# Long runs per partition: stacked operands of the causal attention, and spill and read-back of the relative heads

## The reference, cut to what matters

```
AC = einsum("bhld,bhmd->bhlm", q + u_bias, k)
BD = einsum("bhld,hrd->bhlr", q + v_bias, r)      # r: 2L-1 relative positions
attn = softmax((AC + rel_shift(BD)) / sqrt(8))
```

## Time and profile before

| what | value |
|---|---|
| runs of the kernel, not profiled | 1694.71, 1694.87, 1704.96 us; median 1694.87 us |
| profiled execution | 1699.04 us, of which the span from the first to the last instruction is 1697.2 us |
| PE, DVE, ACT, POOL busy | 87%, 73%, 66%, 26% of the span |
| mean granted TensorE clock | 0.948 of full speed |
| DMA moved | 272.97 MB in 154904 packets |
| causal attention | about 45 to 645 us of the span |
| windowed layers | about 645 to 1150 us |
| relative heads and last feed-forward | about 1150 to 1697 us |

### The profile page before, as it was taken

How to read it: one execution, slowest core, us unless ns; L and a number is a source line. 1 busy time by engine, 2 the same in 40 slices (tenths; PEclk the granted TensorE clock), 3 DMA queues, 4 the chain that set the end, 5 groups by cost and what they waited for, 6 DMA issues and landing times. The chain is left out here.

```text
span 1697.2 us, 36694 instructions
## 1 busy us (share of the span) xinstructions
PE 1473.9 (87%) x12580; PEld 938.1 (55%) x12580; DVE 1234.0 (73%) x3703; ACT 1119.9 (66%) x2657; POOL 440.1 (26%) x442
## 2 busy tenths in 40 slices
PE   4688998989989885588888888769999999999996
PEld 2255555556555553366666666646555555555564
DVE  4367777777777765688888788663877878878755
ACT  1267676776767761567777677627888787887742
POOL 0333333333333313454544444330000000000001
PEclk9599999999999997899999999877999999999998
DMA  1677777788777745111001110007999999999920
GB/s 41 163 185 194 188 186 197 185 194 190 186 186 189 194 108 187 22 30 31 19 20 31 25 27 19 12 13 219 324 315 315 309 314 300 313 314 302 292 73 25
DMA packets 154904, 272.97 MB, mean 161 GB/s; under 512 B 27920, under 2 KB 31200, under 8 KB 154592
## 3 DMA queue, kind: packets, MB, share of 16 engines
q1 hardware_dynamic: 154720, 270.63, 56.3%
HBM read 148.03 MB, written 112.98 MB: 154 GB/s over the span
## 5 line engine op out<-in xcount | busy, mean ns | idle before, releaser
L519 ACT ACTIVATE a_Pm<-a_Pm,a_nm 128x272 f32<-128x272 f32 (+3 forms) x512 | 266.7, 570 | 167.3 <-DVE a_nm L441 166.7
L441 DVE CUSTOM_DVE_ANT_0 a_Pm<-ps,a_mask 128x272 f32<-128x272 f32 (+3 forms) x512 | 237.7, 503 | 92.3 <-PE ps L358 90.8
L1768 ACT COPY r_BD<-ps 128x320 f32<-128x320 f32 x512 | 200.4, 428 | 92.1 <-PE ps L1621 46.7
L1895 DVE CUSTOM_DVE_ANT_0 r_Sx<-ps,r_Sx 128x512 f32<-128x512 f32 x256 | 176.8, 691 | 108.8 <-PE ps L1634 107.2
L1621 PE MATMUL ps<-r_R,r_qv 32*128 32x320 f32 x1024 | 234.2, 498 | 3.2 <-ACT r_BD L1768 2.3
L358 PE MATMUL ps<-a_Kst,a_Qst 128*128 128x272 f32 (+4 forms) x640 | 200.6, 409 | 15.4 <-DMA a_Kst<-bounce 15.1
L1634 PE MATMUL ps<-r_K,r_qu 32*128 32x256 f32 x1024 | 199.7, 436 | 3.4 <-DVE r_nb L1895 3.4
L358 PEld LDWEIGHTS ps<-a_Kst,a_Qst 128*128 128x128 f32 x640 | 113.4, 193 | 146.3 <-issue 62.6
L1775 ACT ACTIVATE r_Sx<-r_Sx,r_nb 128x512 f32<-128x512 f32 x256 | 187.6, 733 | 7.9 <-DVE r_nb L1895 7.9
L1904 DVE COPY r_PT<-ps 128x512 f32<-128x512 f32 x256 | 175.9, 687 | 4.6 <-PE ps L1644 4.0
L373 PE MATMUL ps<-m_ident,a_Pm 128*128 128x128 f32 x1280 | 170.5, 278 | 1.6 <-ACT a_Pm L519 0.7
(11 more groups left out here) (204 smaller groups left out, 2745.9 us busy)
## 6 DMA issues: line engine op xcount, KB each, us to landing
spill<-r_BD SPq DMA_DIRECT2D x256, 288.0 KB, 5.0
r_Sx<-spill SPq DMA_DIRECT2D x128, 512.0 KB, 5.7
a_Kst<-bounce SPq DMA_DIRECT2D x128, 264.0 KB, 4.9
a_Qst<-bounce SPq DMA_DIRECT2D x128, 256.0 KB, 4.6
bounce<-a_kh SPq DMA_DIRECT2D x32, 264.0 KB, 3.5
bounce<-a_kl SPq DMA_DIRECT2D x32, 264.0 KB, 4.1
bounce<-a_qh SPq DMA_DIRECT2D x32, 256.0 KB, 5.7
bounce<-a_ql SPq DMA_DIRECT2D x32, 256.0 KB, 6.0
```

The costliest lines, as they stand in the source:

```text
L441: nc.vector.tensor_tensor_reduce(out=Pm[:, u % 2, qt, 0:w], in0=S[:, S_of[qt]:S_of[qt] + w], in1=mask[:, N + AV - w:N + AV], scale=-SCALE, ...
L519: nc.scalar.activation(row, row, ACT.Exp, scale=-1.0, bias=nm[:, u % 2, qt:qt + 1]).then_inc(exp_done, 1)
L1768: nc.scalar.copy(BD[:, m % BUFS, j, HW * half:HW * half + HW], ps[:, BDB[k % 3], 0:HW]).then_inc(bd_ev, 1)
L1895: nc.vector.tensor_tensor_reduce(out=row, in0=ps[:, AC + n % 2, :], in1=row, scale=-SCALE, scalar=-BIG, op0=ALU.add, op1=ALU.min, accum_ou ...
```

## The change

Both DRAM buffers get a layout in which what one partition reads or writes lies together.

- Stacks: the DRAM buffer is now (2, 32 features, 4 heads, N) and no longer (2, 128, 528). The stacked tiles Qst and Kst have the sequence outside the head. A write goes through a view "c h n -> h c n" of the buffer: its outermost dimension has 4 entries, the next 32. Each of the four reads now has one run of 8192 or 8448 bytes per partition.
- Spill: one DMA writes all 2 x 640 columns of the 128 partitions (5120 bytes each), and the read takes one run of 640 + 512 elements (4608 bytes) per partition. wr rises by 16 instead of 32 per pair. Sx grows to 1152 elements per slot; to make room, yb and the output tile of the norm are laid over the last quarter of xT.
- First keys: first_transposes goes to bank TB + 1 and waits for VectorE's evd instead of ScalarE's eva; the wait for p0_ev moves from the transposes of bank TB (last of a unit) to those of bank TB + 1 (first of a unit).

```diff
-    Qst = [s.sb(f"Qst{i}", [P, GH, NB, N], F32R) for i in range(2)]
-    Kst = [s.sb(f"Kst{i}", [P, GH, NB, KN], F32R) for i in range(2)]
+    Qst = [s.sb(f"Qst{i}", [P, NB, GH, N], F32R) for i in range(2)]
+    Kst = [s.sb(f"Kst{i}", [P, NB, GH, KN], F32R) for i in range(2)]
...
-    bounce = [[nc.dram_tensor(f"bounce{k}{m}", (2, P, KN), F32, kind="Internal").ap() for m in range(4)] for k in range(2)]
+    bounce = [[nc.dram_tensor(f"bounce{k}{m}", (2, AD, GH, (N, KN)[m % 2]), F32, kind="Internal").ap() for m in range(4)] for k in range(2)]
...
-                width_ = (N, KN)[m % 2]
-                    sp.dma_start(bounce[st % 2][m][j, :, 0:width_], src[:, i].bitcast(F32)).then_inc(bounced, 16)
+                    sp.dma_start(bounce[st % 2][m][j].rearrange("c h n -> h c n"), src[:, i].bitcast(F32)).then_inc(bounced, 16)
-                    sp.dma_start(dst[st % 2][32 * block:32 * block + 32, :, i].bitcast(F32),
-                                 bounce[st % 2][m][j, :, 0:width_].rearrange("(h c) n -> c h n", h=GH)).then_inc(stk[st % 2][i], 16)
+                    sp.dma_start(dst[st % 2][32 * block:32 * block + 32, i].rearrange("c h n -> c (h n)").bitcast(F32),
+                                 bounce[st % 2][m][j].rearrange("c h n -> c (h n)")).then_inc(stk[st % 2][i], 16)
...
-                        ins = nc.tensor.matmul(S[:, lo:lo + w], q[:, h, i, P * qt:P * qt + P], k[:, h, i, at:at + w],
+                        ins = nc.tensor.matmul(S[:, lo:lo + w], q[:, i, h, P * qt:P * qt + P], k[:, i, h, at:at + w],
...
+                    if u >= GH and u % GH == 1:
+                        pe.wait_ge(p0_ev, u // GH)
-                if k == 0 and u >= GH and u % GH == 1:
-                    pe.wait_ge(p0_ev, u // GH)
...
-                pe.wait_ge(eva, 2 * min(GH * (bb + 1) + 1, UNITS))
+                pe.wait_ge(evd, min(GH * (bb + 1) + 1, UNITS))
-                    ins = nc.tensor.transpose(ps[:, TB, P * qt:P * qt + P], P0[:, bb % 2, qt, :], c["ident"][:])
+                    ins = nc.tensor.transpose(ps[:, TB + 1, P * qt:P * qt + P], P0[:, bb % 2, qt, :], c["ident"][:])
...
-                nc.vector.tensor_copy(P0T[:], ps[:, TB, :]).then_inc(p0_ev, 1)
+                nc.vector.tensor_copy(P0T[:], ps[:, TB + 1, :]).then_inc(p0_ev, 1)
...
-    def __init__(self, s, name):
+    def __init__(self, s, name, out=None):
-        self.out = s.sb(name + "_out", [P, NT, D])
+        self.out = s.sb(name + "_out", [P, NT, D]) if out is None else out
...
-    spill = [nc.dram_tensor(f"spill{k}", (2, P, BW), F32, kind="Internal").ap() for k in range(SCRATCH)]
+    spill = [nc.dram_tensor(f"spill{k}", (P, 2 * BW), F32, kind="Internal").ap() for k in range(SCRATCH)]
...
-    Sx = s.sb("Sx", [P, SCRATCH, 2, N])
+    Sx = s.sb("Sx", [P, SCRATCH, BW + N])
...
-    yb = s.sb("yb", [P, NT, D])
-    nrm = Norm(s, "n")
+    yb = xT[:, B - 1].rearrange("p (t n) -> p t n", t=NT)
+    nrm = Norm(s, "n", out=yb)
...
-    HW, HP2 = BW // 2, P // 2
+    HW = BW // 2
...
-                    rows_of = spill[k % SCRATCH].rearrange("t p n -> p t n")
-                    sp.dma_start(rows_of[0:HP2, :, HP2:BW], BD[0:HP2, k % BUFS, :, HP2:BW]).then_inc(wr[k % BUFS], 16)
-                    sp.dma_start(rows_of[HP2:P, :, 0:BW - HP2], BD[HP2:P, k % BUFS, :, 0:BW - HP2]).then_inc(wr[k % BUFS], 16)
+                    sp.dma_start(spill[k % SCRATCH], BD[:, k % BUFS].rearrange("p t n -> p (t n)")).then_inc(wr[k % BUFS], 16)
-                    sp.wait_ge(wr[m % BUFS], 32 * (m // BUFS + 1))
+                    sp.wait_ge(wr[m % BUFS], 16 * (m // BUFS + 1))
-                    skew = bass.AP(tensor=a.tensor, offset=P - 1, ap=[[BW - 1, P], [P * BW, 2], [1, N]])
+                    skew = bass.AP(tensor=a.tensor, offset=P - 1, ap=[[2 * BW - 1, P], [1, BW + N]])
...
-                    ins = nc.tensor.transpose(ps[:, TB + n % 2, P * j:P * j + P], Sx[:, n // 2 % SCRATCH, n % 2, P * j:P * j + P],
+                    ins = nc.tensor.transpose(ps[:, TB + n % 2, P * j:P * j + P], Sx[:, n // 2 % SCRATCH, BW * (n % 2) + P * j:BW * (n % 2) + P * j + P],
...
-                    act.wait_ge(wr[m % BUFS], 32 * (m // BUFS))
+                    act.wait_ge(wr[m % BUFS], 16 * (m // BUFS))
-                row = Sx[:, n // 2 % SCRATCH, n % 2, :]
+                row = Sx[:, n // 2 % SCRATCH, BW * (n % 2):BW * (n % 2) + N]
...
-                        act.wait_ge(wr[k], 32 * len(range(k, PAIRS, BUFS)))
+                        act.wait_ge(wr[k], 16 * len(range(k, PAIRS, BUFS)))
...
-                row = Sx[:, m % SCRATCH, n % 2, :]
+                row = Sx[:, m % SCRATCH, BW * (n % 2):BW * (n % 2) + N]
...
-                    nrm.apply(nc, link, nrm.out, yb)
+                    nrm.apply(nc, link, yb, yb)
-                    nc.vector.tensor_tensor(xs, xs, nrm.out[:], ALU.add).then_inc(x_done, 1)
+                    nc.vector.tensor_tensor(xs, xs, yb, ALU.add).then_inc(x_done, 1)
```

## The result

The changed kernel takes 1972.94 us (median of 4 runs, 1968.76 to 1984.96) beside 1698.08 us for the kernel before on the same chip: a ratio of 1.1624, 95% interval 1.1555 to 1.1694. The forecast was 1953 us, slower. In the profiled executions the span goes from 1697.2 to 1967.0 us, +269.8; the forecast had +258.

What follows compares the result with a forecast made beforehand. SP's loop of stack writes, landing and reads was taken to bound the causal attention, TensorE the relative heads. Stack writes +266 us and spill -8 us made +258 on 1694.87, so 1953 us; range 1810 to 2025.

Steps and rivals of the forecast that it cites:

- SP's loop paces the attention, not TensorE: Causal attention: SP's loop of writes, landing and reads sets the stage, 8.98 us a stack; TensorE nearly keeps pace.
- 15.2 us of TensorE's four units: Causal attention: TensorE's time for four units without its stalls, from 17.97 - 1.3 - 1.5.
- The rival at 1600 us: Stacks: writes over 16 engines, reads at 378 GB/s, TensorE then binds: -87 us; chance 0.07.
- Part one: First transposes: the 44 us stall for ScalarE goes but turns into waiting for data; worth 0.
- Part two: Stack reads: runs of 8 KB still fill 32 partitions, so 4.9 us a stack stays; at most 12 us gained.
- the rival of fast reads (1843 us): Stacks: four engines write, but long runs lift reads to 378 GB/s, -110 us; chance 0.13.
- Part three: Stack writes: 4 outermost leaves four engines of 16, +4.23 us a stack, +266 us in all.
- The holes and the clock: Attention: TensorE stands about 10 us a pair and its clock falls, but the longer loop covers it: 0.
- Part four: Relative heads, spill and read: 11.8% more bytes but 376 GB/s, ScalarE's slot wait goes: -8 us (0 to -20).
- a rival with chance 0.06: Relative heads bound by their extra bytes, with four engines for stack writes: +32 us instead of -8, 1993 us; chance 0.06.
- The sum: Whole kernel: 266 - 8 = +258 us, giving 1953 us; chance 0.68 as it stands.
- What was said to show it: Trace signs: SP's write waits doubled, write share 0.25, reads near 217 GB/s, PE about 60%, transposes' stall gone, relative heads shorter.

Runs made afterwards that it cites:

- the last kernel: Kernel before with the first keys' edit and stack reads ordered 0, 64, 32, 96; ScalarE instead of SP issues the bounce writes: 1645.71 us, ratio 0.9706.
- the padded kernel: Kernel before with one padding row per 32 rows in the stacks' DRAM buffer, so writes stay 4 x 32; reads as before: 1964.39 us, ratio 1.1562.
- the series of outermost counts: Stacks' new layout alone on the kernel before, each bounce write as one DMA (4 outermost), two (2) or four (rows): 1954.58, 2280.64, 1741.21 us.

## Why the prediction was right, and where it was not

**SP's loop paces the attention, not TensorE.** Shown. From the first K read to the last the loop grew by 239.7 us and SP's waits for its writes by 239.4. Taking 44 us of stall from TensorE alone moved nothing, and the kernel in which the loop no longer holds the writes ended up bound by TensorE. One number on the way was misread. For the 15.2 us of TensorE's four units the forecast subtracted both rows, 25.9 + 15.1 us, which are largely one wait seen twice, and it subtracted them from the one pair of 17.97, where the mean pair takes 17.7 (548.4 / 31). With the 15.1 alone it is 17.7 - 0.5 - 1.4 = 15.8 us, which the last kernel bears out. The forecast itself doesn't hang on it. The rival at 1600 us and the expectations of three experiments do: they reckoned with up to 2.8 us to gain in a pair, where 1.9 were there.

**Part one at 0.** Shown by the first keys alone: +0.3%, and the stall reappears as a wait for data, as named.

**Part two, reads stay at 4.9 us.** Right on what decides: the reads ran at 235 GB/s with runs of 8 KB, not at 378, and the rival of fast reads (1843 us) fell. The term was 0 and measured -9 (by the ratios, whose intervals overlap) to -19 us (by the stretch).

**Part three, four engines.** Shown by the share (0.26), by the padded kernel and by the series of outermost counts. The terms were a little mis-sized: forecast +4.23 us a stack for the writes and 0 for the reads, measured +3.87 for both, and +249.6 us for all 64 stacks, not +266. The padded kernel parts them: with the old reads it is +4.17 us a stack (806.8 - 548.4 in 62), and the long runs take 0.31 back. So the writes alone came within 0.06 us of the term, and the reads are the rest. In part that is luck. The forecast gave each of the four engines 23.6 GB/s, and four alone moved 100 to 102 GB/s, 25.0 to 25.5 each. 0.532 MB then take 5.2 to 5.3 us instead of 1.41, +3.8 to +3.9; the last 0.3 us of the 4.17 I can't place.

**The holes and the clock at 0.** The granted clock fell from 0.96 to 0.82 in the attention, with stretches at 0.50, the lower of the two levels. PE's busy time rose to 536.8 us, from 476.2 in 70 to 600 of the kernel before, for the same work, and SP's loop covers it: the stage grew by what SP's waits grew. PE's share, forecast at about 60%, was 69: at the lower clock the same work counts as busy for longer.

**Part four, -8 us: wrong, and the step that failed is the rate of the mix.** The forecast took 376 GB/s, seen in a stretch of one microsecond with a read alone, for a stage in which reads and writes run against each other all the time. It had the other number on the page, 323 GB/s (310 at share 0.96), and priced it at 3.86 us a pair and +32 us, as a rival with chance 0.06. Measured: 326 GB/s at share 0.94, that is 347 at full share; 1.245 MB in 3.6 us of a pair of 3.80. So the extra bytes came with a loss of +24.4, beside the main case and not in its place, and near what the rival had priced. Merging the halves did raise the rate, by 7%, and added 11.8% of bytes. The two experiments show that the long write and the long read each carry a part; whether the bandwidth binds or the ring of three slots stays open. "ScalarE waits no more" (64.1 us), "over 340 GB/s" (326) and "5 to 10 us less" (24.4 more) all fell with this step.

**The sum.** 16 us too much in part three and 32 too little in part four, with some 4 given back elsewhere: +12 us, 269.8 where 258 were forecast. The total was near because the errors met, which is luck. The forecast's direction and mechanism rest on part three, which the runs bear out; its closeness to 1972.9 does not.

**What was said to show it.** SP's waits at the same place up 1.8 times, DMA share 0.26 in writes alone, reads at 235 GB/s, the stall before the first transposes gone: as said. The landing time of the bounce writes, said to be 8 to 12 us, has no number in the trace after; SP's longest wait for one, 9.8 us, and 8.7 us in the timeline agree with it.

## What to carry to other kernels

Read the outermost dimension on both sides of each DMA after the views are applied: here 4 in front of 32 on the DRAM side turned 16 engines into 4 and 348 GB/s into 102, while runs four times as long on the other side of the same change were worth 0.5 to 1%. Where the engines' share is already 0.96 over a stage, as here, reckon with the rate of the stage and not of its best microsecond: transfers that were simpler but 11.8% larger made the stage 5% longer. Before adding up an engine's waits, see whether the matmul pipe and its weight loads show the same one twice. In a queue that runs in order, a transfer moved ahead takes its wait for the producer along; here it paid to have one of the engines that make the data send it instead.

## What the runs showed of the hardware

- Few engines alone are no slower each: 25.0 to 25.5 GB/s each of 4 and 25.5 each of 2, against 21.3 to 23.6 for each of 16. The latter are divided by their share; done so, 102 GB/s at 0.26 is 24.5, so whether the few are faster is not clear.
- The order in which reads go to blocks of 32 partitions counts: going 0, 64, 32, 96, K reads of 521.7 us in place of 550.1 (248 GB/s in place of 217 in one window each), and 1.4% of the kernel. Why it helps, and why no more, stays open.
- Reads and writes against each other settled at 310 to 326 GB/s over the whole stage at share 0.94 to 0.96, in five kernels with different run lengths and sizes, while single microseconds of one kind show 376.
